# A graph attention layer on one core: D by row sums while the projections run, c read from PSUM by the exp, c turned on VectorE

## The reference

```python
h = jnp.maximum(_layernorm(x, axis=-1), 0.0)
h = h @ W.T                       # 256 x 256
src = h @ a1; dst = h @ a2
e = leaky_relu(src[:, None] + dst[None, :], 0.2)
e = jnp.where(adj == 0, -9e15, e)
out = x + jax.nn.softmax(e, axis=1) @ h
```

## Time and profile before

| | |
|---|---|
| median of 3 runs | 406.71 us (406.16 to 409.22) |
| profiled execution | span 404.4 us (its time outside the span is not given) |
| PE busy | 390.9 us, 97% |
| DVE busy | 371.7 us, 92% |
| ACT busy | 201.9 us, 50% |
| POOL busy | 69.0 us, 17% |
| chain: PE, DVE, DMA, issue | 68%, 21%, 4%, 3% |
| mean DMA rate | 193 GB/s |

### The profile page before, as it was taken

One profiled execution on the slowest core, in us unless ns is written; L12 is line 12 of the kernel. 1 busy time (PEld: TensorE's weight loads), 2 busy tenths in 40 slices (PEclk: granted clock), 3 DMA queues, 4 the chain that ended last, 5 costly groups with the idle time before them and its releaser, 6 DMA issues.

```text
span 404.4 us, 9752 instructions
## 1 busy us (share of the span) xinstructions
PE 390.9 (97%) x3396; PEld 333.5 (82%) x3396; DVE 371.7 (92%) x457; ACT 201.9 (50%) x291; POOL 69.0 (17%) x73
## 2 busy tenths in 40 slices
PE   7999999899999799999999999999999999999995
PEld 7787678787878588888888888888888888888884
DVE  2999698999999989999998799999998799999965
ACT  3799864545455453444444624445444435544430
POOL 1423055354545212000000021000000120000000
PEclk9999999999999899999999999999999999999998
DMA  7920068555555567766666657666665576666503
GB/s 230 370 78 2 3 208 316 201 195 186 186 192 185 161 204 229 229 217 224 220 220 218 195 167 224 223 220 216 216 222 174 181 225 218 220 220 218 186 0 107
DMA packets 26261, 77.90 MB, mean 193 GB/s; under 512 B 3296, under 2 KB 8960, under 8 KB 26112
## 3 DMA queue, kind: packets, MB, share of 16 engines
q1 hardware_dynamic: 25088, 74.48, 56.6%
q0 software_dynamic: 1152, 3.15, 2.2%
HBM read 73.40 MB, written 4.21 MB: 192 GB/s over the span
## 4 chain that ended last, share of the span: by engine, by line
PE 68%; DVE 21%; DMA 4%; issue 3%; ACT 1%; SPq 1%; DVEq 0%; ACTq 0%
PE ps L819 64%; DVE p_lo L622 9%; DVE p_sb L615 7%; DMA adj_sb<-adj_t 2%; DMA c_flat<-c_turned 1%; DVE stats L495 1%; DMA x_sb<-x 1%; PE ps L781 1%; DVE rows_sb L682 1%; PE ps L766 1%; PE ps L777 1%; PE ps L778 1%; DVE hnt_lo L511 1%; DVE hn_sb L518 1%; ACT hnt_hi L392 0%
## 5 line engine op out<-in xcount | busy, mean ns | idle before, releaser
L819 PE MATMUL ps<-v_sb,p_hi 128*128 (+2 forms) x2048 | 255.0, 273 | 4.0 <-DVE p_lo L622 3.0
L425 ACT ACTIVATE p_hi<-p_sb,p_scale 128x1024 f16<-128x1024 f32 x127 | 145.7, 1149 | 172.1 <-DVE p_sb L615 148.3
L819 PEld LDWEIGHTS ps<-v_sb,p_hi 128*128 128x128 f16 x2048 | 199.0, 97 | 32.8 <-issue 4.4
L622 DVE SCALAR_TENSOR_TENSOR p_lo<-p_sb,p_scale,p_hi 128x1024 f16<-128x1024 f32 x128 | 175.3, 1370 | 9.6 <-ACT p_hi L425 9.6
L615 DVE SCALAR_TENSOR_TENSOR p_sb<-c_row,g_col,adj_sb 128x1024 f32<-128x1024 uint32 (+1 forms) x127 | 162.6, 1282 | 1.6 <-DMA adj_sb<-adj_t 1.6
L819 PE MATMUL ps<-v_sb,p_lo 128*128 (+1 forms) x1024 | 143.5, 274 | 2.1 <-DVE p_lo L622 2.1
L819 PEld LDWEIGHTS ps<-v_sb,p_lo 128*128 128x128 f16 x1024 | 97.7, 98 | 22.2 <-DVE p_lo L622 9.7
L337 POOL TENSOR_TENSOR v_sb<-h_sb,v_sb x32 | 44.0, 1374 | 52.9 <-ACT v_sb L403 52.7
L344 POOL DMA_DIRECT2D out<-rows_sb x24 | 13.2, 551 | 182.0 <-DVE rows_sb L639 180.6
L495 DVE BATCH_NORM_STATS2 stats<-x_sb 128x6 f32<-128x256 f32 x32 | 12.7, 405 | 7.1 <-DMA x_sb<-x 7.1
L331 POOL TENSOR_SCALAR hn_sb<-x_sb,moments,rstd 128x256 f32<-128x256 f32 x8 | 10.7, 1339 | 26.7 <-DVE shift L506 26.7
(11 more groups left out here) (89 smaller groups left out, 114.0 us busy)
## 6 DMA issues: line engine op xcount, KB each, us to landing
adj_sb<-adj_t SPq DMA_DIRECT2D x128, 512.0 KB, 4.8
x_sb<-x SPq DMA_DIRECT2D x8, 512.0 KB, 8.0
out<-rows_sb POOLq DMA_DIRECT2D x24, 128.0 KB, 2.7
c_row<-c_flat SPq DMA_DIRECT2D x1, 1536.0 KB, 6.8
out<-rows_sb SPq DMA_DIRECT2D x8, 128.0 KB, 1.8
w_nat<-w SPq DMA_DIRECT2D x1, 256.0 KB, 2.5
w_f<-w_t SPq DMA_DIRECT2D x1, 256.0 KB, 3.0
a_sb<-a SPq DMA_DIRECT2D x2, 1.0 KB, 2.5
```

The costliest lines, as they stand in the source:

```text
L425: nc.scalar.activation(p_hi[:, u % R, :], p_sb[:, u % R, :], ACT.Copy, scale=p_scale[:, bass.ds(t, 1)])\
L622: nc.vector.scalar_tensor_tensor(out=p_lo[:, u % R, :], in0=p_sb[:, u % R, :], scalar=p_scale[:, bass.ds(t, 1)], in1=p_hi[:, u % R, :], op ...
L819: return nc.tensor.matmul(ps[:, k, 0:width], part[:, u % R, k * P:(k + 1) * P], v_sb[:, bass.ds(t, 1), v, 0:width], start=start, stop=stop ...
```

## The change

- D is found while projections run. d of the last eight tiles (24 to 31) is not read from their projections: VectorE multiplies the normalised tile with a row w2 = W.T a2 and sums (late_d_of), and takes D at tile 25. The row is made by GpSimd, TensorE and ScalarE by tile 14.
- s of the first eight tiles is spread behind tile 20's projection.
- The statistics, the std and the normalises are spread over the tiles by tables; the last statistics come at tile 19.
- ScalarE reads the spread s from PSUM and makes c directly, with D in the exp's bias; t_row and its maximum with 0 are gone (the min with adj cuts at 1 anyway). These exps stand between the relus of tiles 28 to 31; the exp's table is loaded at tile 22. g and p_scale come in two parts.
- VectorE, not ScalarE, copies the projections of tiles 25 to 30 to SBUF.
- The transposes have 3 PSUM banks and not 4.
- c_col is turned by VectorE in 32 x 32 blocks, after the low part of tile 2, and stored by four DMAs of 32 x 32.
- The copies w1_hi, w1_lo move from VectorE to GpSimd; the keep-busy matmuls at the seam go.

```diff
+    LATE_D = 8
+    BY_VECTOR_KEPT = range(T - 7, T - 1)
+    NORMALISE_AT = {t: t - 3 for t in range(3, 12)}
+    for first, at in ((12, 9), (16, 12), (20, 15), (24, 19), (28, 22)):
+        NORMALISE_AT.update({first + i: at + i for i in range(XB)})
+    STD_AT = {1: 1, 5: 2, 8: 3, 11: 4, 14: 5, 18: 6, 21: 7}
+    LATE_D_AT = {T - 10: (24, 25, 26), T - 9: (27, 28), T - 8: (29,), T - 7: (30, 31)}
...
-            sp.wait_ge(c_turned_kept, 1)
-            sp.dma_start(c_flat, c_turned[:]).then_inc(c_flat_stored, 16)
-            sp.wait_ge(c_flat_stored, 16)
+            sp.wait_ge(c_blocks_ready, 1)
+            for b in range(P // T):
+                sp.dma_start(c_flat[:, b * T:(b + 1) * T], c_blocks[b * T:(b + 1) * T, :]).then_inc(c_flat_stored, 16)
+            sp.wait_ge(c_flat_stored, 16 * (P // T))
...
+            def exp_c(m):
+                k0, k1 = FIRST_PARTS[m]
+                bank, column = bank_s + k0 // CT, k0 % CT * P
+                act.wait_ge(s_spread, k0 // CT + 1)
+                nc.scalar.activation(c_row[:, k0 * P:k1 * P], ps[:, bank, column:column + (k1 - k0) * P], ACT.Exp,
+                                     bias=exp_bias[:, 0:1], scale=exp_scale[:, 4:5]).then_inc(c_exp_ready, 1)
...
+                if t == T - 10:
+                    nc.scalar.activation(table_ready[:], eps_sb[:], ACT.Exp)
...
+                if t == T - 5:
+                    values_hi(0)
+                if t == T - 4:
                     act.wait_ge(exp_bias_ready, 1)
+                    exp_c(0)
+                    exp_g(slice(0, BY_VECTOR_KEPT[0]))
+                if t == T - 3:
+                    exp_c(1)
+                if t == T - 2:
+                    exp_c(2)
...
+            def keep_h(t):
+                dve.wait_ge(h_done, t + 1)
+                nc.vector.tensor_scalar(h_sb[:, t, :], ps[:, bank_h + t % 2, 0:FW], H_DOWN, None, ALU.mult)\
+                    .then_inc(h_kept_vector, 1)
...
+                n = t - (T - LATE_D)
+                nc.vector.scalar_tensor_tensor(out=rows_sb[:, n, 0:F], in0=hn_sb[:, t % RN, :], scalar=0.0, in1=w2_row,
+                                               op0=ALU.max, op1=ALU.mult, accum_out=late_d[:, n:n + 1])\
+                    .then_inc(d_most_ready, 1)
...
+                if t == T - 7:
+                    wait_kept(dve, T - LATE_D - 1)
+                    nc.vector.tensor_reduce(late_d[:, LATE_D:LATE_D + 1], h_sb[:, 0:T - LATE_D, F + 1], AX.X, ALU.max)\
+                        .then_inc(d_most_ready, 1)
+                    dve.wait_ge(d_most_ready, LATE_D + 1)
+                    nc.vector.tensor_reduce(d_part[:], late_d[:], AX.X, ALU.max).then_inc(d_part_ready, 1)
...
+                    if u == 3 and first:
+                        dve.wait_ge(c_col_ready, 1)
+                        nc.vector.transpose(c_blocks[:], c_col[:]).then_inc(c_blocks_ready, 1)
...
+                if t == T - 12:
+                    pe.wait_ge(w1_ready, 2)
+                    pe.wait_ge(w2_row_ready, 1)
+                    for m in range(2):
+                        for c in range(KC):
+                            spread_s(m, c)
+                if t == T - 7:
+                    pe.wait_ge(d_part_ready, 1)
+                    nc.tensor.transpose(ps[0:1, bank_d, 0:P], d_part[:], ident[:]).then_inc(d_turned, 1)
+                if t == T - 6:
+                    pe.wait_ge(d_one_ready, 1)
+                    nc.tensor.matmul(ps[:, bank_d, P:P + 1], ones[0:1, :], d_one[:], start=True, stop=True)\
+                        .then_inc(d_spread, 1)
```

More of the change, by code:

```diff
@@ L420, in _ @@
-            act.wait_ge(p_scale_ready, 1)
+                nc.scalar.activation(turned("hi", t), in_chunks(banks_t[t % TB]), ACT.Relu).then_inc(hnt_hi_ready, 1)
+                if t in STD_AT:
+                    std_of(STD_AT[t])
+                if t == T - 10:
+                    nc.scalar.activation(table_ready[:], eps_sb[:], ACT.Exp)
+                for n in BY_SCALAR:
+                    if NORMALISE_AT.get(n) == t:
+                        normalise(n)
+                if t >= 1 and t - 1 not in BY_VECTOR_KEPT:
+                    keep_h(t - 1)
@@ L569, in _ @@
                     link(last)
+                    dve.wait_ge(d_turned, 1)
+                    nc.vector.tensor_reduce(d_one[:], ps[0:1, bank_d, 0:P], AX.X, ALU.max).then_inc(d_one_ready, 1)
+                if t == T - 5:
+                    dve.wait_ge(d_spread, 1)
+                    nc.vector.tensor_scalar(exp_bias[:, 1:2], exp_scale[:, 3:4], ps[:, bank_d, P:P + 1], math.log(P_UP),
+                                            ALU.mult, ALU.add)
+                    nc.vector.tensor_scalar(exp_bias[:, 0:1], exp_scale[:, 0:1], ps[:, bank_d, P:P + 1], None, ALU.mult)\
+                        .then_inc(exp_bias_ready, 1)
+                    link(nc.vector.tensor_copy(d_wide[:], ps[:, bank_d, P:P + 1]))
@@ L609, in _ @@
                     .then_inc(weights_ready if m == len(FIRST_PARTS) - 1 else part_weights_ready, 1)
+            wait_kept(dve, BY_VECTOR_KEPT[-1])
+            wait_kept(dve, T - 1)
+            nc.vector.tensor_scalar(t_col[:], h_sb[:, :, F], d_wide[:, 0:1], 0.0, ALU.add, ALU.max)\
+                .then_inc(t_col_ready, 1)
             dve.wait_ge(p_scale_ready, 1)
@@ L803, in _ @@
                 project(t)
[L805 to L815 removed]
+                if t == 12:
+                    pe.wait_ge(w2_wide_ready, 1)
+                    for c in range(KC):
+                        last = nc.tensor.matmul(ps[:, bank_r, c * P:(c + 1) * P], w2_wide[:, c, :], ident[:],
+                                                start=True, stop=True)
+                    last.then_inc(w2_row_done, 1)
+                if t == T - 12:
+                    pe.wait_ge(w1_ready, 2)
+                    pe.wait_ge(w2_row_ready, 1)
+                    for m in range(2):
+                        for c in range(KC):
+                            spread_s(m, c)
[6 more added lines that the diff above has]
+                        .then_inc(d_spread, 1)
             def product(u, t, k, part, v, start, stop):
@@ L831, in sums @@
                         if k == FIRST_PARTS[-1][0]:
-                            pe.wait_ge(c_col_ready, 1)
-                            nc.tensor.transpose(ps[0:T, RB - 1, turned_c], c_col[:], ident[:]).then_inc(c_all_turned, 1)
                             pe.wait_ge(p_hi_ready, 1)
-                    if first and g is None and k == RB - 1:
-                        pe.wait_ge(c_turned_kept, 1)
+                        if k >= bank_h:
+                            wait_kept(pe, T - 2 + (k - bank_h))
                     if first and g is not None:
```

169 lines of the change are left out of this document (79 added, 90 removed).

## The result

The changed kernel takes 409.01 us (median of 20 runs, 405.89 to 411.47), the one before 406.25 in 20 runs beside them (404.69 to 409.49). The ratio is 1.006, with a 95% interval of 1.0041 to 1.0079: 1.7 to 3.2 us slower, within the 1% that the prediction called no change. The forecast was 408.5.

The account below looks back on a forecast made before the run. VectorE was taken to bound group 0, then 257.51 us of matmuls in groups 1 to 3. First weights 0.6 + t column 0.16 + c 1.0 = +1.8 us on the 406.7 median: 408.5, range 404.2 to 411.2.

Parts of the forecast that it names:

- S: Start of VectorE's low part of tile 20: 32.42 us before the change, forecast at 33.3.
- Tiles 8 to 19: Projections with earlier statistics: VectorE's work sums to 12.5 us and it bounds; S 0.9 later, ends 32.4 and 33.8.
- The spread behind tile 20: 12 spread matmuls, 2.6 us, ahead of tile 23's transposes on TensorE; low part 23 at S+5.0.
- hole: VectorE's idle time before tile 23's low part while TensorE spreads s: 1.5 us, ends 0 and 2.6.
- Row sums: VectorE's sums for d of the last eight tiles: 0.42 us each, five exposed; d_part ready at S+8.75.
- D and its use: From d_part to the first weights: exp_bias at S+11.3, exps delay relus 29 to 31, first weights at S+15.25.
- The column of t: It now lies between tile 0's and tile 1's weights, no longer ahead of both: 0.16 us more.
- c on VectorE: Transpose behind tile 2's low part, then four stores: VectorE's wait at tile 8 1.0 us longer, ends 0.2 and 2.7.
- From group 1 on the same 257 us: Sign of a right forecast: the matmuls of groups 1 to 3 keep their length, 257.51 us before.
- The gain: Rival: tiles 8 to 19 fit 11.7 us, hole filled, weights 1.2 to 2.7 us earlier; 403.5 to 407 us, chance 0.32.
- Slower by over 1%: Rival: c's stores land after about 4.3 us or more and starve tile 8; 410.5 to 413 us, chance 0.14.
- D comes no earlier: Rival: relative to the last projection, since d_one waits for reduces behind tile 25; within the forecast, no separate chance.

Follow-up runs that it names:

- the second: Profile of the changed kernel run once more, unedited, beside others: 409.04 us against 406.26 for the kernel before, ratio 1.0064.
- the first four experiments: Change unedited, tables alone on the kernel before, change with spread in four, change with c turned earlier; kernel before beside them: median 406.26 us (35 runs).
- the next series: Next four: tile 8's edges first in change and in before, tile 30 not held back in before, change without sums; before beside them: median 406.56 us.

## Why the prediction was right, point by point

*Time and verdict.* 408.5 forecast, 409.01 measured; +1.8 forecast from the sum, +2.4 by the distances, +2.8 by the medians. Before's median of three runs, 406.71, on which the forecast stood, was 0.5 above that of twenty; against 406.25 the same sum would have given 408.1. The closeness is in part luck. The stretch before S was forecast 1.5 us too short (2.4 later, not 0.9), what follows S 0.9 too long (0.6 up to the first weights, 0.2 at tile 8), and a base that was 0.5 too high hid part of what remained.

*Tiles 8 to 19: right in kind, too small.* VectorE became the bound there, as the sum of 12.5 us said, and S moved by 2.0 + 0.35, not 0.9. Counted from w_lo that is 34.8 and lies beyond the upper end of 33.8. The tables alone, on the kernel before, show 1.75 of the 2.0. The step that failed is "VectorE no longer waits for anything". The 13.71 us are 1.2 more than the sum: 0.35 is the wait at tile 14 for a relu behind std and normalise (the prediction's upper end had a wait of that kind), 4 x 0.13 go where a statistics and its own aggregate are neighbours (0.45 against the 0.32 taken), and the rest is smaller waits for relus. The 0.32 us were taken from the normalise of the earlier trace rows, where other work stands behind the statistics too, and the tables make the neighbours that those rows do not have.

*The spread behind tile 20: right.* Low part 23 at S+5.05, forecast S+5.0; VectorE's hole 1.70, forecast 1.5. Spread in four, half of it is given back in the distances; the time alone doesn't show how much.

*Row sums: too dear.* 0.34 us each and not 0.42; d_part came at S+8.36, not 8.75. The Trainium skill (VectorE: DVE Perf Modes, "Two Vector instructions with no wait between them") says that such an operation is two instructions, and the trace agrees: the accumulator's read is a row of its own, 0.08 us. But it adds nothing from start to start (38.56 to 38.90), so the 0.45 us that the prediction worked out by that rule did not come. Leaving out seven sums gave 0.69 us, where five of them lie outside the hole: VectorE was the bound there for less than half of them.

*D and its use: right in order, 0.4 to 0.6 us early, most of it at d_part already.* exps from S+10.8 (forecast 11.3), relus of 29 to 31 at S+11.9, 12.6, 13.5 (forecast 12.4, 13.1, 14.1), first weights at S+14.61 (forecast 15.25). The nearer weights make up less than half of what S was late: first weights behind w_lo +1.4, forecast +0.6.

*The column of t:* +0.16, as forecast.

*c on VectorE: right in kind, a little too dear.* Stores issued where forecast, the last after 2.25 us (taken 2.5), tile 8 later by 0.77 (forecast 1.0), and gone once the edges leave first. The Trainium skill (DMA: Bandwidth & Descriptors, Specifications) says that transfers below 512 B are done as read-modify-write. That decided nothing here: four stores in rows of 128 B landed faster, 1.8 us on the median, than the one in rows of 512 B before, 4.29. No run here stores the same bytes in both ways with the queue empty, so what the rule costs stays open.

*From group 1 on the same 257 us:* not in the first profile (258.64), but in the second (257.31); it goes with the clock, which was low for 6.8 us in the first and for 3.4 in the second, as in the kernel before. I had not seen that the clock falls behind the 3 us gap at the end of group 0, although its rows were there.

*The rivals.* The gain did not come: S was 2.4 us later, and the hole stayed. Slower by over 1% did not come: no store took 4 us. "D comes no earlier" was wrong: the first exp with D starts 3.9 us ahead of the first weights (47.08, 50.93), where before it was 1.7 (46.25, 47.96), but ScalarE's and VectorE's work in between makes that worthless.

*Open.* The times put the change 0.4 us higher than its distances do. It may be the clock, which was full in 5 of the change's 20 runs, with a mean of 406.9 us, and lower in the others: the four runs of before with the clock full in the first four experiments have 404.4, and 2.5 us between the two is what the distances say. But it is not all of the scatter, since two of the four full-clock runs of before in the next series took 406.1 and 406.3 us, and two 404.2 and 404.3. Why the clock falls behind a gap in some runs and not in others, and why for 3.4 or for 6.8 us, is not shown.

## What to carry to other kernels

Work moved out of a serial seam is free only where its new neighbours are idle: count the busy time of all engines in the stretch that receives it, and add what neighbours on one engine wait for each other, since a forecast from start-to-start times alone came out 1.2 us short here, in a stretch of 13.7 us of which VectorE is busy 94%. Before a seam is rebuilt, look in the chain for transfers that share a queue with the work's own loads, and for TensorE gaps that a wait for two tiles makes: here two edits of a few lines, an order of DMAs and a wait for one tile instead of two, were worth 3.4 us, and the rebuilt seam less than nothing. And set two profiles side by side only as distances from a common point, since one load of x alone moved them by 1.5 us.
